# Graph network on one core: smaller one-hots and another zeroing queue in setup, PSUM tiles and plain maxima in the second layer

## The reference, cut to what matters

```python
for r in range(R):                       # 4 relations
    mask = (edge_type == r)[:, None]
    h = (x @ W[r]).reshape(N, H, D)
    e = leaky_relu(e_src + e_dst, 0.2)   # per edge and head
    e_max = maximum(segment_max(where(mask, e, -1e30), dst), 0.0)
    e_exp = where(mask, exp(e - e_max[dst]), 0.0)
    alpha = e_exp / (segment_sum(e_exp, dst)[dst] + 1e-8)
    out += segment_sum(alpha[:, :, None] * h[src], dst)
```

## Time and profile before

| | us |
|---|---|
| median of 3 runs | 4879.8 (4876.2 to 4903.41) |
| the profiled execution | 4879.92 |
| its span | 4878.2 |

### The profile page before, as it was taken

How to read it: one execution, slowest core, us unless ns; L and a number is a source line. 1 busy time by engine, 2 the same in 40 slices (tenths; PEclk the granted TensorE clock), 3 DMA queues, 4 the chain that set the end, 5 groups by cost and what they waited for, 6 DMA issues and landing times. The chain is left out here.

```text
span 4878.2 us, 58266 instructions
## 1 busy us (share of the span) xinstructions
PE 2067.6 (42%) x11828; PEld 1169.3 (24%) x11828; DVE 3684.8 (76%) x7145; ACT 2658.1 (54%) x5774; POOL 3352.6 (69%) x2937
## 2 busy tenths in 40 slices
PE   2499999999851000000000300000000159898885
PEld 1255545444431000000000200000000025555553
DVE  9566656556457998999897868888888757777776
ACT  0388878788631877777775222222222146665663
POOL 0488888888717777777773467777777427777775
PEclk9899999999976555555555555555555579999998
DMA  9655555555533666666665356666666413333332
GB/s 401 196 100 108 102 100 101 100 100 100 117 77 126 223 259 245 256 255 242 256 253 220 92 184 216 215 216 216 211 213 215 131 43 116 125 123 121 116 125 85
DMA packets 281725, 817.19 MB, mean 168 GB/s; under 512 B 62406, under 2 KB 177622, under 8 KB 269523
## 3 DMA queue, kind: packets, MB, share of 16 engines
q1 hardware_dynamic: 99250, 506.75, 27.8%
q0 software_dynamic: 169776, 248.56, 23.4%
q10 hardware_dynamic: 12528, 60.37, 3.0%
HBM read 366.96 MB, written 448.51 MB: 167 GB/s over the span
## 5 line engine op out<-in xcount | busy, mean ns | idle before, releaser
L627 POOL DMA_INDIRECT tab<-arena x560 | 947.5, 1692 | 208.3 <-issue 137.1
L1542 PE MATMUL psum<-ident,arena 128*128 128x128 f32 x15 | 3.7, 428 | 2220.4 <-DVEq L1570 2220.4
L757 PE MATMUL psum<-arena 128*128 128x512 bf16 (+1 forms) x4704 | 943.5, 355 | 0.0
L1894 POOL DMA_INDIRECT arena<-table,arena x784 | 751.2, 958 | 242.6 <-issue 238.7
L1311 POOL DMA_INDIRECT arena<-table,arena x588 | 652.9, 1110 | 185.3 <-issue 171.7
L2383 POOL DMA_INDIRECT arena<-table,arena x622 | 605.9, 974 | 205.1 <-issue 182.2
L2469 PE MATMUL psum<-arena 128*128 128x512 bf16 x4050 | 676.4, 329 | 90.1 <-DVE arena L2502 48.9
L1358 ACT ACTIVATE arena<-arena 128x128 f32<-128x128 f32 x1680 | 505.4, 387 | 159.7 <-DVE arena L1470 157.2
L1470 DVE SCALAR_TENSOR_TENSOR arena<-arena 128x512 f32<-128x512 f32 x728 | 544.2, 747 | 12.1
L757 PEld LDWEIGHTS psum<-arena 128*128 128x128 bf16 x4704 | 432.0, 99 | 469.0 <-issue 16.4
L1542 PEld LDWEIGHTS psum<-ident,arena 128*128 128x128 f32 x15 | 2.7, 213 | 2220.9 <-DVEq L1570 2220.7
(11 more groups left out here) (414 smaller groups left out, 4770.9 us busy)
## 6 DMA issues: line engine op xcount, KB each, us to landing
rows<-arena SPq DMA_DIRECT2D x56, 3808.0 KB
arena<-seg_rows SPq DMA_DIRECT2D x112, 896.0 KB, 6.8
rows<-arena SPq DMA_DIRECT2D x56, 1008.0 KB
seg_rows<-arena ACTq DMA_DIRECT2D x28, 1792.0 KB
rows<-arena SPq DMA_DIRECT2D x56, 896.0 KB, 3.7
arena<-table,arena POOLq DMA_INDIRECT x1994, 3.1
arena<-src_lanes SPq DMA_DIRECT2D x56, 448.0 KB
tab<-arena POOLq DMA_INDIRECT x560
```

What stands on the lines that cost most here:

```text
L627: eng.indirect_dma_start(out=m.tabs[j], out_offset=bass.IndirectOffsetOnAxis(ap=idx[g][:, k:k + 1], axis=0), in_=rows[g][:, k, 0:D], in_of ...
L757: t = eng.matmul(ps[:, c, 0:w], part[n // 2 % PAIRS][:, n % 2, :], hot[n % HOTS][:, lo:lo + w], start=False, stop=False, skip_group_check= ...
L1894: eng.indirect_dma_start(out=kv[k][:, j, :], out_offset=None, in_=m.table2, in_offset=bass.IndirectOffsetOnAxis(ap=idx[k][:, j:j + 1], axi ...
```

## The change

In setup, the digits become 64 and 50 wide: one-hots are 14 x 64 and 14 x 50, the degrees come out in halves and are put together by two more matmuls and one more copy. The 28 zeroing DMAs go from ScalarE's queue to SyncE's, behind the load of x, and the four of `tabs` go there too, now behind all other zeros. ScalarE's own work comes ahead of its 33 small loads.

In the second layer the columns 8 to 13 of `apart` lie in PSUM banks 2 to 7 (one bank for each), `weight` moves into the banks of `ex`, the first scores are loaded and summed in four parts in place of two, and the reduction becomes two maxima of two inputs.

```diff
@@ setup_phase
+            @block.sync, after the loads of x and wait(const, 18)
+                eng.wait_ge(l_dst, 48)
+                with eng.Fori(0, TURNS) as i:
+                    eng.dma_start(lanes(m.seg_rows)[...], zeros).then_inc(zeroed, 16)
                 ... the six fills, the store of src_lanes ...
+                eng.wait_ge(zeroed, 16 * ZEROS)
+                for j in range(TABS):
+                    eng.dma_start(m.tabs[j][0:NP, :]..., zeros[:, 0:NB * D]).then_inc(tabs_zeroed, 16)
@@ scalar: the same two loops taken out; conversions and copies out of PSUM now ahead of the small loads
@@ tensor
-                eng.matmul(ps[:, 7, 0:NB], nul, nul[:, 0:NB], start=False, stop=True).then_inc(deg_done, 1)
+                eng.matmul(degrees, nul[:, 0:LOW], nul[:, 0:HIGH], start=False, stop=True).then_inc(halves_done, 1)
+                eng.wait_ge(prep, S_HALVES)
+                for k in range(2):
+                    t = eng.matmul(ps[k * LOW:(k + 1) * LOW, 5, 0:NB], m.ident[0:LOW, 0:LOW], by_two[:, k, :], start=True, stop=True)
+                t.then_inc(deg_done, 1)
@@ vector
-                        eng.tensor_tensor(hot_lo[h], spread(iota, 1, [P, HALF, P]), ...
+                        eng.tensor_tensor(hot_lo[h], spread(iota[:, 0:LOW], 1, [P, HALF, LOW]), ...
-                        eng.tensor_tensor(hot_hi[h], spread(iota[:, 0:NB], 1, [P, HALF, NB]), ...
+                        eng.tensor_tensor(hot_hi[h], spread(iota[:, 0:HIGH], 1, [P, HALF, HIGH]), ...
+                eng.wait_ge(halves_done, 1)
+                assert step(eng.tensor_copy(deg_half[0:LOW, :], ps[0:LOW, 7, 0:HIGH])) == S_HALVES
+LOW, HIGH = 64, 2 * NB
@@ layer1_edges
+IN_PSUM = 6
-        apart = A(HALF, REL * D)
+        apart_sb = A(HALF - IN_PSUM, REL * D)
+        apart = [apart_sb[:, t, :] if t < HALF - IN_PSUM else m.psum[:, 8 - HALF + t, :] for t in range(HALF)]
-        weight = m.psum[:, 2, 0:APART * H1]...
+        weight = [m.psum[:, h, RH * COLS:RH * COLS + APART * H1]... for h in range(2)]
+        PARTS = 4
-                for c in range(2):
+                for c in range(PARTS):
                     (load and running sums of one part of the first scores)
-                f.then(eng.tensor_reduce(ed, ed_all.rearrange("p t (r a) -> p t a r", a=H1), AX.X, ALU.max))
+                two = ed_all[:, :, 0:2 * H1]
+                eng.tensor_tensor(two, two, ed_all[:, :, 2 * H1:RH], ALU.max).then_inc(ed_steps, 1)
+                eng.wait_ge(ed_steps, PARTS * RH + 2)
+                f.then(eng.tensor_tensor(ed, ed_all[:, :, 0:H1], ed_all[:, :, H1:2 * H1], ALU.max))
                     v.put(eng.scalar_tensor_tensor(out=row[:, j, 0:SUM], in0=..., scalar=keeps[h][:, j:j + 1],
-                                                       in1=apart[:, j, :], op0=ALU.mult, op1=ALU.add))
+                                                       in1=apart[j], op0=ALU.mult, op1=ALU.add))
```

More of the change, by code:

```diff
@@ L218, in setup_phase @@
         lane_base = A(1)
-        hot_lo = [A(HALF, P, dt=BF16) for _ in range(2)]
-        hot_hi = [A(HALF, NB, dt=BF16) for _ in range(2)]
+        hot_lo = [A(HALF, LOW, dt=BF16) for _ in range(2)]
+        hot_hi = [A(HALF, HIGH, dt=BF16) for _ in range(2)]
+        deg_half = A(HIGH)
         deg, tot, incl, end1, tmp, ones_nb = (A(NB) for _ in range(6))
@@ L330, in _ @@
                 eng.dma_start(w_nat[:, LIN2:SLOTS, :], I["L2_gnn_lin2_w"].rearrange("o (j i) -> o j i", i=P)).then_inc(l_w, 16)
[L331 to L345, removed]
                 eng.wait_ge(l_src, 48)
@@ L363, in _ @@
                     eng.activation(m.xT[:, c:c + w], ps[:, k % 2, 0:w], ACT.Copy).then_inc(xt_kept, 1)
+                for c, name in enumerate(COLUMNS):
+                    eng.dma_start(m.cols[:, c:c + 1], I[name].rearrange("(p a) -> p a", a=1), allow_slow_non_contiguous=True).then_inc(l_small, 16)
+                eng.dma_start(m.lin1_b[:, :], I["L2_gnn_lin1_b"].rearrange("(j p) -> p j", p=P), allow_slow_non_contiguous=True).then_inc(l_small, 16)
+                for r, name in enumerate(ROWS):
+                    eng.dma_start(m.rows[:, r, :], I[name].partition_broadcast(P)).then_inc(l_small, 16)
+                eng.dma_start(m.w_rel[:, :, :], I["L1_gnn_W"].rearrange("r i o -> i r o")).then_inc(l_small, 16)
+                for k, (name, at) in enumerate((("L3_gnn_Wm", 0), ("L3_gnn_Wm", D), ("L3_gnn_W1", 0), ("L3_gnn_W1", D), ("L3_gnn_W2", 0))):
+                    eng.dma_start(m.w3[:, k, :], I[name][at:at + D, :]).then_inc(l_small, 16)
+                eng.dma_start(m.edge_w[:, :], I["L3_gnn_Wm"][2 * D, :].partition_broadcast(P)).then_inc(l_small, 16)
                 eng.wait_ge(l_small, 16 * SMALL)
[L366 to L370, removed]
             @block.tensor
@@ L492, in _ @@
                 eng.wait_ge(whole_done, 1)
-                step(eng.tensor_scalar(m.whole_neg[:, :], ps[:, 5, 0:P], -1.0, BIG, ALU.add, ALU.mult))
+                step(eng.tensor_scalar(m.whole_neg[:, :], ps[:, 5, P:2 * P], -1.0, BIG, ALU.add, ALU.mult))
 SRCB = 112
-S_DEG = 7
-S_START = 16
-S_WHOLE = 20
+LOW, HIGH = 64, 2 * NB
+S_HALVES = 7
+S_DEG = 8
+S_START = 17
+S_WHOLE = 21
+assert 2 * LOW == P and HIGH <= P
 ZEROS = TURNS + 6
@@ L1236, in layer1_edges @@
         sums = [A(RH, COLS) for _ in range(2)]
-        weight = m.psum[:, 2, 0:APART * H1].rearrange("p (t a) -> p t a", a=H1)
+        weight = [m.psum[:, h, RH * COLS:RH * COLS + APART * H1].rearrange("p (t a) -> p t a", a=H1) for h in range(2)]
         score4 = A(HALF, H1)
@@ L1246, in layer1_edges @@
         SUM, MAX = REL * D, REL * D + RH
-        ed_in, ed_first_in = [sem(f"dst_scores_landed{c}") for c in range(2)], sem("first_scores_landed")
+        PARTS = 4
+        ed_in, ed_first_in = [sem(f"dst_scores_landed{c}") for c in range(PARTS)], sem("first_scores_landed")
         begun, ed_steps = sem("buffers_begun"), sem("dst_scores_steps")
@@ L1357, in set_apart @@
                         for r in range(REL):
-                            eng.activation(apart[:, t, r * D:(r + 1) * D], feat[k][:, t, 0:D], ACT.Copy, scale=hot[k % 2][:, t, r:r + 1]).then_inc(masked, 1)
+                            eng.activation(apart[t][:, r * D:(r + 1) * D], feat[k][:, t, 0:D], ACT.Copy, scale=hot[k % 2][:, t, r:r + 1]).then_inc(masked, 1)
                 def turn(i, last):
@@ L1395, in _ @@
                 eng.wait_ge(ed_first_in, 16)
-                for c in range(2):
-                    t0, t1 = c * T // 2, (c + 1) * T // 2
+                for c in range(PARTS):
+                    t0, t1 = c * T // PARTS, (c + 1) * T // PARTS
                     eng.wait_ge(ed_in[c], 16)
                     if c:
-                        eng.wait_ge(ed_steps, RH)
+                        eng.wait_ge(ed_steps, RH * c)
                     for k in range(RH):
```

39 lines of the change are left out of this document (23 added, 16 removed).

## The result

The changed kernel takes **4806.0 us** (median of 4 runs, 4805.0 to 4811.3) beside 4883.4 us (4876.2 to 4903.4) of the kernel before, a ratio of 0.984 with a 95% interval of [0.981, 0.987]. The forecast was 4813. The profiled execution takes 4805.2 us and its span is 4803.5, 74.7 us less than before. By starts of phases in the two traces that is: setup -7.9, the layer between +2.4, the gathers before the loop -0.9 (as measured from the start of that layer), the loop -57.3 (the stretch of the earlier trace rows runs 0.1 us past the end of its last gather), from the last gather to the last step -5.0, and the later layers -6.0.

What follows compares the result with a forecast made beforehand. The prediction took GpSimd's gathers, held up by VectorE instructions with two SBUF inputs, to bound the second layer's loop. From 4879.9 us it took 15 (setup), 1 (before the loop) and 51 (loop): 4813 us, range 4778 to 4850.

Steps and rivals of the forecast that it cites:

- The loop: Second layer's loop: PSUM inputs in steps 8 to 13 stop holding up gathers, -51 us, bounds -26 and -83.
- Setup: Setup: earlier scatter start, shorter scatter run and shorter tail, together -15 us, bounds -17 and -7.
- the -4.6 that was forecast: Setup's scatter: VectorE's setup work no longer holds up its early instructions, -4.6 us, bounds 0 and 4.6.
- The term that failed: Setup: scatter starts at 140.5 us, when the zeros end, 9.6 us earlier than before.
- if the zeros end past 146 us: Setup: one of the signs in the profile after by which the prediction would be wrong.
- its bounds of 0 to +6: Setup: later end of the zeros when issued behind x on SyncE's queue, +0.5 us taken, bounds 0 and +6.
- Before the loop: Second layer ahead of the loop: VectorE 12.4 us earlier but maxima block GpSimd, -1 us, bounds -4 and +4.
- Rival A: Loop: any long dense VectorE run holds gathers up, they stay at 1.086 us; 4865 us, chance 0.08.
- Rival D: VectorE's chain in the loop: PSUM makes VectorE slower, kernel slower than before at 4921 us; chance 0.03.
- Rival B: Loop: gathers lock onto the eight SBUF steps left, -26 us, setup -10; 4844 us, chance 0.14.
- Rival C: Loop: all gather excess goes and VectorE becomes the bound, -84 us; 4781 us, chance 0.07.
- Rival E: Setup: zeros start only after x has crept through, scatter 41 us later, +36 us; 4864 us, chance 0.03.

Runs made afterwards that it cites:

- e1: Kernel before with only the six PSUM columns (and `weight` beside `ex`): ratio 1.009 against the kernel before on its own chip.
- e5: Kernel before with only the six PSUM columns, again on a second chip: ratio 1.024 against the kernel before there.
- e10: Kernel before with only the six PSUM columns, again on a third chip: ratio 1.024 against the kernel before there.
- e2: Kernel before with the new setup alone, `layer1_edges` as before: ratio 0.999 against the kernel before.
- e3: Kernel before with only the maxima and the first scores in four parts, `weight` beside `ex`, no column in PSUM: ratio 0.995 against the kernel before.
- e4: Changed kernel with the 28 zeroing DMAs back on ScalarE's queue, ahead of its own work: ratio 1.000 against the kernel before.
- e12: Changed kernel with the six small fills ahead of the 28 zeros on SyncE's queue: 4786.8 us, ratio 0.981 against the kernel before.
- e11: Kernel before, unchanged, run for its trace on the fourth chip: 4888 us.
- e9: Whole changed kernel, unedited, on the third chip: 5888.5 us beside 5776.7 for the kernel before, ratio 1.019.
- e6: Changed kernel with columns 2 to 7 in PSUM in place of 8 to 13: ratio 1.008 against the kernel before.
- e7: Changed kernel with columns 3, 7, 9, 11, 12 and 13 in PSUM: ratio 1.009 against the kernel before.

## Why the prediction was right, and where it was not

The time was inside the range and near the forecast, but as a sum of a loop that gained more and a setup that gained half.

- **The loop: -51 forecast, -57.3 measured.** The mechanism is as told: PSUM inputs free the gathers beside them (1.27 to 1.37 us down to 0.95), e1, e5 and e10 show that these columns alone do it, and e2 and e3 that the other parts don't, all on chips where the gathers are not the bound. The gather is at 1.007 us (1.01 forecast), the half at 18.4 (18.5), VectorE idle 39 us (35). The sum left an excess of 1.93 - 0.98 = 0.95 us a half over the free gather; measured are 14 x (1.007 - 0.948) = 0.83, since only two gathers of a half are held. That is the 6 us.
- **Setup: -15 forecast, -7.9 measured.** The scatter's own run, 185.38 - 150.14 = 35.2 us between first and last before and 178.72 - 148.07 = 30.7 after, gave the -4.6 that was forecast, and the tail behind it -1.2 for -0.8. The term that failed is the first: -9.6 for an earlier start, where it was -2.1. It took the end of the zeros from the bandwidth in the earlier trace rows, between 139 and 140 us. Four things make up the 7.6 us from 140.5 to 148.07. In the trace before the last 14 KB packet ends at 143.97 us, 3.5 us behind the forecast start, which the positions hid there. In the changed kernel it ends 1.1 us later, at 145.06. The fills, now on the same queue, take the late engine another 1.2 us, to 146.31. And from there to the scatter's start there are 1.8 us (1.5 in e4 and e12, from the last 14 KB packet), where the forecast had nothing. The prediction's own mark, "if the zeros end past 146 us", is just passed if the fills are counted, by 0.3 us; the large zeros alone end before it. The loss by the move, 2.2 us, lies within its bounds of 0 to +6. The size of the gain has some play too: the old setup ends between 192.6 and 194.0 us in its traces (before, e1, e11), the new one between 184.5 and 186.1 (e2, e12, after).
- **Before the loop: -1 forecast, -0.9 measured**, with gathers of 6.43 and 3.15 us beside the maxima (7 and 4 forecast), and no idle time at the first gather of the loop.
- **The rest, not forecast:** -5.0 us behind the last gather and -6.0 us in later layers. e11 against the trace before, the same kernel, is 3.7 us shorter in the first and 5.3 us longer in the second, so most of this is no gain of the change.
- **Rival A** (the lock is not in the inputs) is refuted by the gathers at 0.95 us beside PSUM steps. The box on blocked DMAs in the Trainium skill ("SBUF — State Buffer", section "SBUF: two separate sides") names only two-port perf-mode instructions; here fp32 additions and maxima of two SBUF inputs hold a gather for 13.53 and 6.43 us, and the measurement decides. The same section also names a VectorE instruction with two SBUF inputs, against a GpSimd instruction that reads SBUF, and with that the trace agrees.
- **Rival D** (PSUM makes VectorE slower) is refuted by 746 ns beside 743. The dearer PSUM source of the Trainium skill ("VectorE: DVE Perf Modes", the section on the TRN2 errata) doesn't show in this instruction.
- **Rival B** (the phases move) happened in a mild form: two SBUF steps meet a gather in each half, 104 held gathers in all for 276 before.
- **Rival C** (VectorE becomes the bound) didn't happen in the changed kernel, but e12 comes close to it: 17.84 us a half, VectorE idle for 14.9 us where it was 84 before, 4786.8 us for the 4781 worked out. Not all excess is gone there: one gather in each half is still held, 14 x (0.970 - 0.948) = 0.31 us. Its chance of 0.07 looks too low, since it hung on where the gathers lock and not on the eight steps as such.
- **Rival E** is refuted: x takes 3.98 us of SyncE's queue before the first zero at 18.18 us.

Not foreseen by any case: on a chip of the other kind the same change makes the kernel 1.9% slower (e9). On the two others of that kind its variants are at 1.000 (e4) and 1.008 to 1.009 (e6, e7). That the time came out within 7 us of the forecast is partly luck: the setup brought 7 us less and the first layer cost 2.4, while the loop brought 6 us more and the stages behind it 11 that nobody forecast.

## What to carry to other kernels

Where software-issued gathers run beside long VectorE instructions with two SBUF inputs, moving one input to PSUM frees the gathers, here at 3 ns of VectorE a step; how much comes of it depends on which of the remaining steps a gather meets, and that can lock into one of two rhythms half a microsecond apart in every half. The end of a large transfer is its completion, not the end of its bandwidth: look at the last microseconds with a low share of the DMA engines, and at everything that stands on the same queue before the semaphore is full. And the same edit can gain on one chip and lose on another, so a gain at the gathers counts only where they are the bound.

## What the runs showed that was not expected

- Four chips of two kinds. On three of them the kernel before takes 5760 to 5809 us, on the fourth 4877 to 4899. All phases are alike up to some 1490 us of the span. From there, ScalarE and VectorE get their instructions at times only every 1.4 us, in stretches such as the 13 us shown above. The stretch itself, and the one behind it, in which ScalarE is on time again and GpSimd still waits:

```profile
2055.00:2068.00 13.00, 0.00 (x0) 0.00 (x0) 3.58 (x6) 3.56 (x10) 9.29 (x10) 0.50 0.27 78
2068.00:2076.00 8.00, 0.00 (x0) 0.00 (x0) 6.55 (x11) 6.37 (x23) 0.00 (x0) 0.50 0.00 0
```

While the instructions are late the DMA engines are busy for 27% only, where the loop of the changed kernel has 72% without such lateness, so it isn't a fight for DMA engines. The cause, and why kernels with PSUM columns have about twice as many of these stretches, stays open; the kernel before was timed on such a chip but left no trace there.
- The end of the 28 large zeros isn't even: one DMA engine writes its last packets of 14 KB one by one, some 4 to 5 us after most others have ended, on whichever queue they are issued (143.97 us before, 144.39 in e4, 145.06 in the changed kernel).
- At a tie of 0.09 us between one step and one gather, in the second half of the loop, two traces part that end 27.5 us apart in the loop's length.
